# A fused two-layer Perceiver block on one core: one run of P times V per unit of the second cross-attention, and shared gate and up products in three fp32r passes

## What is computed

```
x += cross_attention(ln(x), ctx)        # layer 0, first 64 context rows, 16 heads of 32
x += causal_self_attention(ln(x))       # layer 0
x += moe(ln(x)) + shared_mlp(ln(x))     # 64 experts, top 8 in 4 of 8 groups; 512 -> 352 -> 512
x += cross_attention(ln(x), ctx, mask)  # layer 1, 1601 context rows per batch
x += causal_self_attention(ln(x))       # layer 1
x += int8_matmul(ln(x))                 # layer 1
shared_mlp(x) = (silu(x @ Sg.T) * (x @ Su.T)) @ Sd.T      # 704 hidden, held as two halves of 352
```

## Time and profile before

| | us |
|---|---|
| median of 3 runs | 1648.01 (1646.71 to 1651.56) |
| profiled execution | 1653.6, of it 1651.8 in the span |
| PE busy | 1599.3 (97%) |
| PEld busy | 1406.2 (85%) |
| DVE busy | 1096.3 (66%) |
| ACT busy | 821.3 (50%) |
| POOL busy | 465.2 (28%) |

### The profile page before, as it was taken

One profiled execution on the slowest core, in us unless ns is written; L12 is line 12 of the kernel. 1 busy time (PEld: TensorE's weight loads), 2 busy tenths in 40 slices (PEclk: granted clock), 3 DMA queues, 4 the chain that ended last, 5 costly groups with the idle time before them and its releaser, 6 DMA issues.

```text
span 1651.8 us, 35385 instructions
## 1 busy us (share of the span) xinstructions
PE 1599.3 (97%) x13652; PEld 1406.2 (85%) x13653; DVE 1096.3 (66%) x2217; ACT 821.3 (50%) x1248; POOL 465.2 (28%) x421
## 2 busy tenths in 40 slices
PE   8999999999999999899999999999999999999897
PEld 5666688888888888769999999999999999999583
DVE  3878787787787788655656556565565655656666
ACT  1242177777777777324545445454354544634122
POOL 3012134444544544231413214132041320410100
PEclk9999999999999999999999999999999999999999
DMA  8003399999999999400202002020020100201200
GB/s 308 7 2 122 105 369 337 336 341 343 344 328 339 330 335 314 128 6 3 79 7 81 6 2 81 7 81 7 1 81 7 61 26 2 81 2 42 94 27 26
DMA packets 68858, 214.63 MB, mean 130 GB/s; under 512 B 13618, under 2 KB 31282, under 8 KB 58880
## 3 DMA queue, kind: packets, MB, share of 16 engines
q1 hardware_dynamic: 54400, 196.03, 34.1%
q0 software_dynamic: 14336, 16.83, 4.5%
HBM read 207.81 MB, written 21.76 MB: 139 GB/s over the span
## 4 chain that ended last, share of the span: by engine, by line
PE 81%; DMA 9%; DVE 5%; issue 2%; ACT 1%; SPq 1%; POOL 0%; ACTq 0%; DVEq 0%; POOLq 0%
PE PS L1352 17%; PE PS L1343 17%; PE PS L2233 10%; PE PS L1387 6%; PE PS L1368 6%; PE PS L2259 4%; PE PS L1410 3%; PE PS L400 3%; PE PS L2255 3%; PE PS L458 2%; DMA qbd<-in_w_gu 2%; DMA S<-in_w_gu 2%; DMA R<-in_w_gu 2%; PE PS L421 1%; PE PS L755 1%
## 5 line engine op out<-in xcount | busy, mean ns | idle before, releaser
L1352 PE MATMUL PS<-S_r 128*128 128x256 f32 x2496 | 319.4, 282 | 0.0
L1352 PEld LDWEIGHTS PS<-S_r 128*128 128x128 f32 x2496 | 309.7, 188 | 3.4 <-issue 0.5
L1343 PE MATMUL PS<-S_r 128*128 128x384 f32 (+1 forms) x1536 | 306.5, 349 | 0.0
L1539 DVE SCALAR_TENSOR_TENSOR kq<-PS,bias_c,kq 64x384 fp32r<-64x384 f32 (+1 forms) x256 | 162.3, 634 | 206.7 <-ACT kq L1470 201.9
L1343 PEld LDWEIGHTS PS<-S_r 128*128 128x128 f32 x1536 | 268.3, 188 | 6.5 <-issue 0.5
L2233 PE MATMUL PS<-S_r,R_r 128*128 128x352 f32 x1152 | 273.5, 328 | 0.2 <-DVE R_r L2387 0.2
L1470 ACT ACTIVATE kq<-PS,bias_c 64x384 fp32r<-64x384 f32 (+1 forms) x256 | 151.1, 590 | 197.1 <-PE PS L1343 193.7
L2233 PEld LDWEIGHTS PS<-S_r,R_r 128*128 128x128 f32 x1152 | 198.6, 188 | 3.8 <-DVE R_r L2387 0.5
L2180 POOL DMA_INDIRECT moe_acc<-x,cols x64 | 125.0, 1953 | 220.2 <-ACT x L2318 130.3
L1280 POOL COPY S<-qbd 64x128 f32<-64x128 f32 x128 | 38.3, 299 | 486.0 <-PE PS L1368 467.2
L1261 POOL TENSOR_TENSOR S_r<-S,S_r 128x1536 fp32r<-128x1536 f32 (+2 forms) x31 | 116.9, 3781 | 130.9 <-ACT S_r L1461 107.7
(11 more groups left out here) (250 smaller groups left out, 2610.6 us busy)
## 6 DMA issues: line engine op xcount, KB each, us to landing
R<-in_w_gu SPq DMA_DIRECT2D x34, 1408.0 KB, 16.7
R<-in_w_dna SPq DMA_DIRECT2D x50, 512.0 KB, 17.2
qbd<-in_w_gu SPq DMA_DIRECT2D x16, 1408.0 KB
S<-in_w_gu SPq DMA_DIRECT2D x16, 1408.0 KB
S<-in_ctxT SPq DMA_DIRECT2D x24, 768.0 KB, 4.7
R<-in_w_dnb SPq DMA_DIRECT2D x50, 192.0 KB, 18.7
xnT<-in_w_dna SPq DMA_DIRECT2D x16, 512.0 KB
S<-in_ctxT SPq DMA_DIRECT2D x8, 898.0 KB
```

The costliest lines, as they stand in the source:

```text
L1343: last = nc.tensor.matmul(PS[:, bank, 0:n], w3[0][:, cc, f0:f0 + P], x3[i][:, cc, 0:n], start=(cc == 0 and w3 is wkv_hi and x3 is ctx_hi), ...
L1352: last = nc.tensor.matmul(PS[:, bank, 0:256], x3[need][:, cc, k0:k0 + P], w3[1][:, cc, f0:f0 + 256], start=(cc == 0 and w3 is wkv_hi and x ...
L1539: nc.vector.scalar_tensor_tensor(out=k[other, 0:n], in0=PS[r, bank_of(b, dc, ("k", c)), 0:n], scalar=bias_c[r, 3, f:f + 1], in1=k[r, 0:n]. ...
```

## The change

Two parts. In the second cross-attention `z0 P0 P1 P2 P3` stand together at the end of every unit, and the turned probabilities get four pairs of buffers. In the shared stage the gate and up products of row tiles 1 to 3 (`k` 2 to 7, twelve groups of the sixteen) are made in three fp32r passes. ACT makes the high parts of rows and weights, POOL the rests, in the order `SH_LO`. The rows' high parts of tile 1 lie where `xn` was, so ACT waits for the store of `xn` first; the first expert's high parts share a buffer with the shared weights', so they move behind `sh_u` 7.

```diff
+        sgu_hi = [wgu_hi[0], Arena(kq[:, :]).view(NC, 2, I)]
+        sgu_lo = wgu_lo[2:4]
+        xs_hi = [None, Arena(S_r, 14200).view(NC, P)] + [Arena(flat4(qbd_r), NC * 2 * I + i * NC * P).view(NC, P)
+                                                          for i in range(2)]
...
+        pTx += [[vbias[:, :].rearrange("p (a b) -> p a b", a=4), wbd],
+                [Arena(R1, 2 * NC * SP + 4 * P + p * P).view(1, P) for p in range(2)]]
...
+        SH_LO = [("x", 1), (0, 0), (0, 1), ("x", 2), (1, 0), (1, 1), ("x", 3)]
...
+            def shared_rows_low(t):
+                pool.wait_ge(sh_hi, (2, 4, 5)[t - 1])
+                nc.gpsimd.tensor_tensor(xnT_r[:, :, tile(t)], xnT[:, :, tile(t)], xs_hi[t].bitcast(F32),
+                                        ALU.subtract).then_inc(sh_lo, 1)
+
+            def shared_low(hf, gu):
+                pool.wait_ge(sh_hi, 1 if hf else 3)
+                pool.wait_ge(sh_u if gu else sh_g, hf + 1)
+                nc.gpsimd.tensor_tensor(sgu_lo[hf][:, :, gu, :], wgu[2 + hf][:, :, gu, :],
+                                        sgu_hi[hf][:, :, gu, :].bitcast(F32), ALU.subtract).then_inc(sh_lo, 1)
+
+            pool.wait_ge(lg_made, 1)
+            for piece in SH_LO:
+                if piece[0] == "x":
+                    shared_rows_low(piece[1])
+                else:
+                    shared_low(*piece)
...
-                for c in range(NC):
-                    last = nc.tensor.matmul(PS[:, 2 + 2 * hf + gu, 0:I], xnT[:, c, t * P:(t + 1) * P],
-                                            wgu[2 + hf][:, c, gu, :], start=(c == 0), stop=(c == NC - 1))
+                if k < 2:
+                    for c in range(NC):
+                        last = nc.tensor.matmul(PS[:, 2 + 2 * hf + gu, 0:I], xnT[:, c, t * P:(t + 1) * P],
+                                                wgu[2 + hf][:, c, gu, :], start=(c == 0), stop=(c == NC - 1))
+                else:
+                    pe.wait_ge(sh_lo, max(SH_LO.index(("x", t)), SH_LO.index((hf, gu))) + 1)
+                    lo = xnT_r[:, :, t * P:(t + 1) * P]
+                    for c in range(NC):
+                        for x3, w3 in ((xs_hi[t], sgu_hi[hf]), (lo, sgu_hi[hf]), (xs_hi[t], sgu_lo[hf])):
+                            last = nc.tensor.matmul(PS[:, 2 + 2 * hf + gu, 0:I], x3[:, c, :], w3[:, c, gu, :],
...
+            def shared_high(hf):
+                nc.scalar.copy(sgu_hi[hf], wgu[2 + hf]).then_inc(sh_hi, 1)
+
+            def shared_rows_high(t):
+                nc.scalar.copy(xs_hi[t], xnT[:, :, tile(t)]).then_inc(sh_hi, 1)
...
             probs_c(1, 3)
+            act.wait_ge(ld_sh, 96)
+            shared_high(1)
             z_c(1, 3)
...
+            act.wait_ge(rows_out, 32)
+            act.wait_ge(xT_ready, 3 * NT)
+            shared_rows_high(1)
+            shared_high(0)
             shared_silu(0)
+            shared_rows_high(2)
+            shared_rows_high(3)
...
             shared_ht(act, 5)
+            shared_silu(6)
+            act.wait_ge(sh_u, 2 * NT - 1)
             weights_high(0, 0)
-            shared_silu(6)
             shared_silu(7)
...
+            shared_mul(6)
             weights_low(0, 0)
-            shared_mul(6)
             shared_mul(7)
...
-        SEQ = ["v0 k0 T0 k1 s0 v1 T1 k2 s1 v2 z0 P0 P1 T2 k3 s2 v3 v4 T3 s3 v5 v6 P2 P3",
-               "v7 k0 T0 k1 s0 v8 T1 k2 s1 v9 z0 P0 P1 T2 k3 s2 v10 v11 T3 s3 P2 P3",
-               "k0 k1 T0 s0 k2 T1 s1 k3 z0 P0 P1 T2 s2 T3 v12 s3 P2 P3",
-               "v0 v1 k0 v2 T0 k1 s0 v3 v4 T1 k2 s1 v5 v6 v7 z0 P0 P1 T2 k3 s2 v8 v9 v10 T3 s3 v11 v12 P2 P3"]
+        SEQ = ["v0 k0 T0 k1 s0 v1 T1 k2 s1 v2 T2 k3 s2 v3 v4 T3 s3 v5 v6 z0 P0 P1 P2 P3",
+               "v7 k0 T0 k1 s0 v8 T1 k2 s1 v9 T2 k3 s2 v10 v11 T3 s3 z0 P0 P1 P2 P3",
+               "k0 k1 T0 s0 k2 T1 s1 k3 T2 s2 T3 v12 s3 z0 P0 P1 P2 P3",
+               "v0 v1 k0 v2 T0 k1 s0 v3 v4 T1 k2 s1 v5 v6 v7 T2 k3 s2 v8 v9 v10 T3 s3 v11 v12 z0 P0 P1 P2 P3"]
...
-                                                pTx[tg % 2][g // 2][0:n, i, S1 * (g % 2):S1 * (g % 2) + S1],
+                                                pTx[tg][g // 2][0:n, i, S1 * (g % 2):S1 * (g % 2) + S1],
...
+                    if isinstance(r, int) and r == 0 and k == 0:
+                        act.wait_ge(sh_u, 2 * NT)
```

More of the change, by code:

```diff
@@ L242, in perceiver @@
                 for i in (2 * turn, 2 * turn + 1)] for turn in range(2)]
+        pTx += [[vbias[:, :].rearrange("p (a b) -> p a b", a=4), wbd],
+                [Arena(R1, 2 * NC * SP + 4 * P + p * P).view(1, P) for p in range(2)]]
+        assert 2 * NC * SP + 6 * P <= 14200
         mx4 = sb("mx4", [P, 2, 4])
@@ L280, in perceiver @@
         wbd_ready = sem("wbd_ready"); zpad_set = sem("zpad_set"); rix_ready = sem("rix_ready"); dve_x = sem("dve_x")
-        dve_seq3 = sem("dve_seq3"); dve_seq4 = sem("dve_seq4"); pool_seq4 = sem("pool_seq4")
+        dve_seq3 = sem("dve_seq3"); dve_seq4 = sem("dve_seq4");
         ff_x = sem("ff_x"); ff_y = sem("ff_y")
@@ L285, in perceiver @@
         eot_made = sem("eot_made"); tables = sem("tables"); n_ready = sem("n_ready"); rows_out = sem("rows_out"); acc_out = sem("acc_out")
-        sh_g = sem("sh_g"); sh_u = sem("sh_u"); sh_silu = sem("sh_silu"); sh_h = sem("sh_h")
+        sh_hi = sem("sh_hi"); sh_lo = sem("sh_lo"); sh_g = sem("sh_g"); sh_u = sem("sh_u"); sh_silu = sem("sh_silu"); sh_h = sem("sh_h")
         sh_t = sem("sh_t"); sh_ht = sem("sh_ht"); sh_d = sem("sh_d"); sh_y = sem("sh_y")
@@ L753, in shared_in @@
                     pe.wait_ge(sh_h if gu else sh_silu, k - 1)
-                for c in range(NC):
-                    last = nc.tensor.matmul(PS[:, 2 + 2 * hf + gu, 0:I], xnT[:, c, t * P:(t + 1) * P],
-                                            wgu[2 + hf][:, c, gu, :], start=(c == 0), stop=(c == NC - 1))
+                if k < 2:
[8 more added lines that the diff above has]
+                            last = nc.tensor.matmul(PS[:, 2 + 2 * hf + gu, 0:I], x3[:, c, :], w3[:, c, gu, :],
+                                                    start=(c == 0 and x3 is not lo and w3 is sgu_hi[hf]),
+                                                    stop=(c == NC - 1 and w3 is sgu_lo[hf]))
                 last.then_inc(sh_u if gu else sh_g, 1)
@@ L1489, in turned @@
                 act.wait_ge(ptx_made, 8 * u + 2 * tg + 1)
-                nc.scalar.copy(pTx[tg % 2][0][0:n, :, :].rearrange("p a b -> p (a b)")[:, 0:w],
+                nc.scalar.copy(pTx[tg][0][0:n, :, :].rearrange("p a b -> p (a b)")[:, 0:w],
                                PS[0:n, 2, 0:w]).then_inc(ptx_act, 1)
@@ L1583, in turned @@
                 dve.wait_ge(ptx_made, 8 * u + 2 * tg + 2)
-                nc.vector.tensor_copy(pTx[tg % 2][1][0:n, :, :].rearrange("p a b -> p (a b)")[:, 0:w],
+                nc.vector.tensor_copy(pTx[tg][1][0:n, :, :].rearrange("p a b -> p (a b)")[:, 0:w],
                                       PS[0:n, 3, 0:w]).then_inc(ptx_dve, 1)
```

## The result

The changed kernel takes **1658.7 us** (median of 5 runs, 1657.6 to 1660.2) against 1649.6 for the kernel before on the same chip: a ratio of **1.0051, interval [1.0036, 1.0066]**, or 9 us slower. Its profiled execution took 1660.2 us, of it 1658.3 in the span; the one of before took 1653.6 and 1651.8.

The account below looks back on a forecast made before the run. DVE's router chain was taken to bound the shared stage until the last table, TensorE after it and in the second cross-attention. Shared stage +12.2 and units +2.2 on 1648.0 gave 1662.4 us; forecast case 1655 to 1667, 8-in-10 range 1643 to 1670.

Parts of the forecast that it names:

- ACT's queue: Shared stage: silu behind the rows' store and two copies delays `shared_mul(0)` by 5.8 us, 1.3 comes back, net 4.5.
- POOL against DVE: Router in the shared stage: POOL's subtractions block DVE's steps for 15.3 us against 5.8 now, 9.5 us more.
- Behind the last table: Shared stage, TensorE alone: four of the twelve cheaper product groups lie there, 1.8 us gained.
- TensorE sets everything: Rival, shared stage and units: DVE's chain has room, so 5.4 and 6.2 us are gained, 1636.4 us; chance 0.13.
- POOL doesn't shut DVE out further: Rival, shared stage: it changes by only 2.7 us, giving 1652.9 us; chance 0.17.
- The clock: Rival, shared stage: TensorE's longer waits lower the granted clock, 4.6 us of lost work, 1667.0 us; chance 0.12.
- Clean units: Second cross-attention, 23 units of `dc` 0, 1 and 3: the joined run gains 0.20 us each, 4.6 us.
- Units of `dc` 2: Second cross-attention, eight units: `T3` waits for `T2`'s copies, 0.85 us longer each, 6.8 us lost.

Follow-up runs that it names:

- silu_first: The changed kernel with `shared_silu(0)` put ahead of ACT's wait for the store of the rows; 1657.5 us, ratio 1.0042.
- rest_late: The kernel before with POOL's two key/value subtractions moved behind the first gathers; 1647.1 us, ratio 0.9978.
- silu_late: The changed kernel with `shared_silu(0)` ahead of ACT's wait and POOL's two key/value subtractions behind the first gathers; 1654.9 us, ratio 1.0030.

## Why the prediction was right

The forecast was 1662.4 us, within 1655 to 1667 for its own case; 1658.7 came. Its sum was +14.4 us: +12.2 in the shared stage and +2.2 in the units. Measured by stages: +10.1, and -0.3 in the units less their last wait, 9.8 in all. So the sum was 4.6 us too large, and both terms erred to the same side; the forecast lay on a median of before of 1648.0, where 1649.6 was measured beside the changed kernel, and this takes 1.6 of the difference away by luck. The shared stage's mechanism held; of the units' 2.2 us of loss nothing came. The medians differ by 9.1 (interval 5.9 to 10.9), the two profiled executions by 6.6 only, since the experts' stage, the last wait and the tail happened to be 1.2, 1.1 and 0.7 us shorter in that of the changed kernel and its shared stage began 0.4 earlier.

**ACT's queue: right.** `shared_mul(0)` was to stand 5.8 us longer; from the first shared product it is 142.16 - 129.67 = 12.49 against 6.83 in before, 5.7. The store landed at 137.2 (137.7), the two copies took 0.62 and 2.53 us (0.6 and 2.6), the table load stayed directly ahead of silu, 1.28. The 1.27 us in front of `shared_mul(1)` came back as said. That DVE really lost this time is one matter, whether it cost the kernel another: silu_first shows that without it the chain only runs into POOL earlier, and 0.7 us remain. With the seven subtractions cut short, the same edit gives 2.5 us (66.66 to 64.11). The term was right in size for this kernel and wrong as a price of its own.

**POOL against DVE: the mechanism right, the term too large.** 15.3 us were counted, 13.3 measured; against 5.8 in before that is 7.5 more, not 9.5. With ACT's term this closes the stretch to the last table: 5.7 - 1.3 + 7.5 = 11.9, and 11.87 were measured. All seven steps that were hit are the ones named, now lines 1122, 1123, 1127, 1138, 1140, 1146 and 1148: 0.8, 2.9, 0.6, 0.9, 2.9, 1.3 and 3.8 us, where 1.0, 3.2, 0.8, 1.2, 3.2, 1.7 and 4.2 were put. POOL's own times were right (6.33 and 6.51 us for two of 1408 elements, 3.2 each). Each hit is 0.2 to 0.4 us short of them, since at a change-over both engines show work for a moment: DVE's line 1123 runs to 146.85, POOL's next subtraction starts at 146.65. I had priced seven hits without that. The Trainium skill (SBUF — State Buffer, Who interferes with whom) says that whoever issues first holds the shared ports for its whole instruction and the other is fully blocked. The trace agrees, and shows what that does to a chain of small steps: even one on 128x4 elements stood 3.76 us. What it doesn't show is that POOL's work is paid in full: some 26 us of it beside the chain cost 13.3.

**Behind the last table: right.** 1.8 us were to be won, 1.75 were. Gate groups of twelve go in steps of 1.92 us.

**The rivals.** *TensorE sets everything* fell in the shared stage, by the 5.70 us that DVE idles and by its longer steps, and in the 8 units of `dc` 2 by `T3`'s waits; in the other 23 it held. *POOL doesn't shut DVE out further* fell by 13.3 against 5.8, and rest_late shows that even the 5.8 cost 4.4 us up to the first expert. By its number, 1652.9, it would lie below the measured range.

**The clock: its condition came, its price didn't.** The stretches of the changed kernel (clock in the third column from the end):

```profile
142.00:148.80 6.80, 6.01 (x17) 4.83 (x18) 6.50 (x7) 2.46 (x7) 6.80 (x4) 0.50 0.00 0
148.80:155.70 6.90, 4.29 (x20) 2.91 (x18) 6.80 (x15) 2.57 (x4) 6.90 (x3) 0.99 0.00 0
155.70:169.30 13.60, 8.94 (x32) 7.39 (x33) 13.32 (x10) 1.56 (x1) 11.21 (x3) 0.50 0.01 1
```

The grant fell to 1.2 GHz while TensorE stood ahead of `shared_turned(0)` (3.39 us) and again while it stood ahead of the ranks (7.27); it was there from 142.0 to 148.8 and from 155.7 to 169.3: the twenty rank matmuls took 4.53 us in place of 2.44. On the whole kernel it cost nothing that can be seen: from `shared_mul(0)` to the last table DVE has no wait for TensorE in the timeline, and TensorE waits for DVE at the second and the last table (0.79 and 0.58 us), as long as in before. The 11.87 us are also accounted for without it. Where TensorE sets the stage alone it does cost, as in silu_late.

**Clean units: the term was too small.** 0.20 us each was a choice between 0.14 and 0.26; it was 0.29, so 6.7 us in place of 4.6. The fixed part read from the earlier trace rows, 0.14, holds (104 instructions take 1.59 us, 64 take 1.03 and 40 take 0.70), so the neighbours' share is as large again, 0.15, where I had allowed 0.06. The timelines show it on both sides of the run: from `s3` to what follows it 0.90 us in place of 1.00 in `dc` 1, and 0.79 in place of 0.85 for the `T2` that stood behind `P1`.

**Units of `dc` 2: right.** 0.79 us longer each, 0.85 forecast. `v12` begins 0.28 us earlier in the unit, where 0.15 was forecast, and from there the unit takes 1.07 us longer; DVE's copy is the last that `T3` waits for, as said. The waits of `T3` sum to 0.98 us per unit, where 1.3 were named.

**Not taken from the profile:** the 5.8 us of shut-outs in the kernel before stood in the earlier trace rows and in the sum, as something already paid. That most of it could be had back for one moved loop, 4.4 us to the first expert and 3.1 on the median, came only from the runs.

## To carry to other kernels

Where a chain of small DVE steps sets a stage, subtractions on POOL that read SBUF are paid for with a good part of their length (here 13.3 of 26 us, and 5.1 to 8.6 of 9), and taking one cause away moves the shut-outs to other steps: move POOL's list as a whole to a place where no chain runs, and look again for who stands there (the 11.24 us of silu_late). Joining two short runs of another tile shape gained 0.29 us here for each pair joined where the copies stay covered; where the run was itself the cover of a copy, leave it split in those units alone. Read what an old kernel pays by the same mechanism before adding to it.

## What the runs showed of the hardware

- A DVE step of four elements takes 0.17 us alone and up to 4.42 us while POOL subtracts 2048 elements; a cast of 32 elements went to 2.95. Reductions beside the same subtractions keep their time to a few per cent (3.66 us in before with POOL idle, 3.66 for line 1142 in the changed kernel, 3.82 in silu_first).
- Right behind a run of 104 matmuls that start every 13.9 ns, TensorE stood 3.42 us with no wait of the program in one unit, and 0.8 in another, in two kernels at the same units and in no other kernel with the same run. Packets of the instruction queues landed in the longer stop. Its condition stays open.
- The granted clock fell to 1.2 GHz in waits of TensorE of 3.4, 7.3 and 6.4 us. The first two cost nothing that can be seen, beside a chain on DVE that was later anyway; the third cost 2.8 us, where TensorE set the stage alone.
- The wait of the first product behind the units for a load varies from 0.2 to 2.8 us between executions, and the experts' stage by some 5: single profiles of this kernel can't tell less than that, while stretches without loads repeat to 0.03 us (59.35 to 59.38 to the last table in four kernels).
